# Zero fill of the sorted rows moved from the first stage into the first attention, and context values projected in blocks of 128 rows instead of 77

## What is computed

```python
x = x + xattn0(ctx, ctx, layernorm(x), mask)      # 16 heads of 32, weights shared by the heads
x = x + bit_linear_conv_ffn(layernorm(x))
x = x + xattn1(layernorm(x), ctx, ctx)            # 16 heads of 64
x = x + moe(layernorm(x))                         # tokens sorted by expert, two per token

# inside both cross attentions
K = ctx @ Wk.T ;  V = ctx @ Wv.T                  # 616 = 8*77 context rows
out = softmax(Q @ K.T * scale) @ V @ Wo.T

# inside moe
x_sort = x_flat[token_ids_sort]
w13_out = ragged_dot(x_sort, moe_w13, group_sizes)
```

## Time and profile before

| what | value |
|---|---|
| three runs | 3473.69, 3482.69, 3483.56 us |
| span of the profiled execution | 3475.7 us |
| `context` | 0 to 157 us |
| `attention` 0 | 157 to 644.7 us |
| PE busy / DVE busy, whole kernel | 2708.8 / 1980.7 us |
| PE busy in the last 26 us of `context` | 0.00 us |

### The profile page before, as it was taken

One profiled execution on the slowest core, in us unless ns is written; L12 is line 12 of the kernel. 1 busy time (PEld: TensorE's weight loads), 2 busy tenths in 40 slices (PEclk: granted clock), 3 DMA queues, 4 the chain that ended last, 5 costly groups with the idle time before them and its releaser, 6 DMA issues. The chain is left out here.

```text
span 3475.7 us, 44833 instructions
## 1 busy us (share of the span) xinstructions
PE 2708.8 (78%) x14170; PEld 1390.6 (40%) x14171; DVE 1980.7 (57%) x2814; ACT 1157.9 (33%) x1751; POOL 934.7 (27%) x739
## 2 busy tenths in 40 slices
PE   7578888446656647888888831999999999999980
PEld 4245555212222214444555310454444445444440
DVE  3287777689999996666666463223333332333225
ACT  2133333266656535555555332111111111111110
POOL 0001010046756751111111025002233350550007
PEclk9789999678877878999999775999999999999995
DMA  9800000100000010000000145001222230320018
GB/s 383 130 30 6 11 5 8 49 0 1 1 0 0 1 51 9 8 8 11 7 7 8 37 145 179 31 30 61 72 69 82 86 107 30 103 91 30 30 43 275
DMA packets 146005, 194.13 MB, mean 56 GB/s; under 512 B 85073, under 2 KB 85073, under 8 KB 145417
## 3 DMA queue, kind: packets, MB, share of 16 engines
q1 hardware_dynamic: 120569, 102.96, 10.6%
q0 software_dynamic: 25360, 90.21, 7.5%
HBM read 122.65 MB, written 70.48 MB: 56 GB/s over the span
## 5 line engine op out<-in xcount | busy, mean ns | idle before, releaser
L1789 PE MATMUL e_gate_up<-weights,e_x_t 128*128 x3456 | 771.5, 380 | 1.4 <-ACT e_x_t L1843 1.4
L1789 PEld LDWEIGHTS e_gate_up<-weights,e_x_t 128*128 128x128 bf16 x3456 | 332.6, 98 | 377.0 <-issue 4.3
L1876 DVE TENSOR_TENSOR e_mid<-e_gate,e_gate_up 128x512 f32<-128x512 f32 x144 | 99.0, 687 | 644.0 <-ACT e_gate L1849 644.0
L1809 PE MATMUL e_out<-weights,e_mid_t 128*128 x1728 | 384.7, 379 | 1.1 <-DVE e_mid_t L1889 1.1
L1849 ACT ACTIVATE e_gate<-e_gate_up 128x512 f32<-128x512 f32 x144 | 86.0, 597 | 684.0 <-PE e_gate_up L1789 684.0
L546 PE MATMUL a_turn<-a_wo,a_mixed_t 128*128 128x512 bf16 (+1 forms) x1024 | 284.2, 434 | 2.3 <-DVE a_mixed_t L804 1.7
L1035 PE MATMUL f_product<-f_xq_t,f_w 128*128 128x512 bf16 x512 | 168.2, 468 | 118.7 <-DVE f_padded L1236 89.9
L1809 PEld LDWEIGHTS e_out<-weights,e_mid_t 128*128 128x128 bf16 x1728 | 169.1, 98 | 204.8 <-issue 1.2
L479 POOL TENSOR_TENSOR a_probs<-a_e,a_probs 128x616 bf16<-128x616 f32 x64 | 85.6, 1353 | 545.1 <-ACT a_probs L713 545.1
L989 POOL TENSOR_TENSOR f_shared<-f_shared 128x512 f32<-128x512 f32 x128 | 180.8, 1413 | 171.0 <-DVE f_shared L1268 171.0
L978 POOL TENSOR_TENSOR hidden<-hidden,f_up_row 128x512 f32<-128x512 f32 x128 | 199.1, 1565 | 88.2 <-ACT f_up_row L1181 88.2
(11 more groups left out here) (234 smaller groups left out, 4485.5 us busy)
## 6 DMA issues: line engine op xcount, KB each, us to landing
raw_weights<-in_w POOLq DMA_DIRECT2D x72, 512.0 KB, 4.0
sorted_x<-c_zero_row POOLq DMA_DIRECT2D x1, 18432.0 KB
e_x_rows<-sorted_x SPq DMA_DIRECT2D x72, 256.0 KB, 2.7
sorted_y<-e_y_rows SPq DMA_DIRECT2D x72, 256.0 KB, 2.0
raw_weights<-in_w SPq DMA_DIRECT2D x24, 512.0 KB, 4.1
x<-in_x SPq DMA_DIRECT2D x4, 2048.0 KB, 49.1
out<-x SPq DMA_DIRECT2D x32, 256.0 KB, 4.2
hidden<-in_w_t SPq DMA_DIRECT2D x1, 4096.0 KB, 13.6
```

Of the source, the lines that this page charges most:

```text
L1789: last = nc.tensor.matmul(gate_up[half][:, part, :], x_t[:, u, a, k, :], plan.weights13[:, bass.ds(expert % 2, 1), b, k, col:col + 512], s ...
L1809: last = nc.tensor.matmul(out[:, :], mid_t[:, a, j, :], plan.weights2[:, bass.ds(expert % 2, 1), b, j, :], start=(j == 0 and a == b == 0), ...
L1876: nc.vector.tensor_tensor(mid[:, half, :], gate[:, half, :], gate_up[half][:, 1, :], ALU.mult).then_inc(mid_made, 1)
```

## The change

There are two edits in `context` and one in `attention` 0.

The zero row, the fill and the wait for it leave `context`. In `attention` 0 POOL clears its own `zero_row` behind its two other memsets, adds the bias to the eight tiles of batches 0 and 1, issues the fill, adds the bias to the other 24 tiles and waits for the fill at its end.

The values of a layer are computed in blocks over the 616 rows of all batches: four of 128 and one of 104, where there were eight of 77. The list `products` has 13 entries of layer 0 (16 before) and 26 of layer 1 (32 before). Each block of values is stored when its last column piece is done: five stores where there was one for layer 0, and five for each of the two parts in layer 1.

```diff
-    values = [sb("values0", [KEYS, B, CH[0] * P]), sb("values1", [KEYS, 2, B, CH[1] * P], BF16)]
+    values = [sb("values0", [P, BLOCKS, CH[0] * P]), sb("values1", [P, 2, BLOCKS, CH[1] * P], BF16)]
...
-            for b in range(B):
+            for r in range(BLOCKS):
                 for lo in range(0, CH[n] * P, 512):
-                    products.append(("values", n, b, lo, lo + 512))
+                    products.append(("values", n, r, lo, lo + 512))
...
-                elif kind == "values" and i == B - 1 and hi == CH[n] * P:
+                elif kind == "values" and hi == CH[n] * P:
                     wait_out(sp, u)
                     for a in parts:
-                        source = values[0][:, :, :] if a is None else values[1][:, a, :, :]
-                        target = values_out[0] if a is None else values_out[1][a]
-                        sp.dma_start(target.rearrange("b k n -> k b n"), source).then_inc(stored, 16)
+                        source = values[0][:, i, :] if a is None else values[1][:, a, i, :]
+                        target = (values_out[0] if a is None else values_out[1][a]).rearrange("b k n -> (b k) n")
+                        sp.dma_start(target[i * P:i * P + rows_of(i), :], source[0:rows_of(i), :]
+                                     ).then_inc(stored, 16)
                         made += 1
             sp.wait_ge(stored, 16 * made)
-            sp.wait_ge(cleared, 16)
...
-            nc.gpsimd.memset(zero_row[:, :], 0.0).then_inc(zeroed, 1)
-            pool.wait_ge(zeroed, 5)
-            pool.dma_start(sorted_x.rearrange("(s p) d -> p s d", p=P),
-                           zero_row[:, :].unsqueeze(1).broadcast_to([P, SLOTS, 2 * D])).then_inc(cleared, 16)
...
-                        last = nc.tensor.matmul(out[0:KEYS, :], ctx_t[:, k, i * KEYS:(i + 1) * KEYS],
+                        last = nc.tensor.matmul(out[0:rows_of(i), :], ctx_t[:, k, i * P:i * P + rows_of(i)],
                                                 wv[:, k, lo:hi], start=(k == 0), stop=(k == KD - 1))
...
+                nc.gpsimd.memset(zero_row[:, :], 0.0).then_inc(row_zeroed, 1)
                 pool.wait_ge(small_in, 16)
-                with pool.Fori(0, NT) as t:
+
+                def add_bias(t):
                     pool.wait_ge(xn_made, t + 1)
                     nc.gpsimd.tensor_tensor(core.x[:, t, :], core.x[:, t, :], bo[:, :], ALU.add
                                             ).then_inc(bo_added, 1)
+
+                for t in range(2 * TPS):
+                    add_bias(t)
+                pool.wait_ge(row_zeroed, 1)
+                pool.dma_start(w["sorted_x"].rearrange("(s p) d -> p s d", p=P),
+                               zero_row[:, :].unsqueeze(1).broadcast_to([P, SLOTS, 2 * D])).then_inc(cleared, 16)
+                with pool.Fori(2 * TPS, NT) as t:
+                    add_bias(t)
+                pool.wait_ge(cleared, 16)
```

More of the change, by code:

```diff
@@ L127, in norm_on_act, with context @@
     nc.scalar.activation(core.norm_tmp[:, 1, :], core.norm_tmp[:, 0, :], ACT.Sqrt).then_inc(root_ready, 1)
-def context(nc, core, x_in, w, keys_out, values_out, sorted_x):
+def context(nc, core, x_in, w, keys_out, values_out):
     QUARTERS = 4
@@ L140, in context @@
     BANKS = 8
+    FULL_BLOCKS, REST = divmod(BK, P)
+    BLOCKS = FULL_BLOCKS + 1
     with ExitStack() as stack:
@@ L146, in context @@
         ctx_t = sb("ctx_t", [P, KD, BK])
-        zero_row = sb("zero_row", [P, 2 * D], BF16)
         wk4 = sb("wk4", [DH, 4, DH])
@@ L155, in context @@
         keys = [sb("keys0", [P, CH[0], BK]), sb("keys1", [P, 2, CH[1], BK], BF16)]
-        values = [sb("values0", [KEYS, B, CH[0] * P]), sb("values1", [KEYS, 2, B, CH[1] * P], BF16)]
+        values = [sb("values0", [P, BLOCKS, CH[0] * P]), sb("values1", [P, 2, BLOCKS, CH[1] * P], BF16)]
         x_in_sb = [sem(f"x_in{q}") for q in range(QUARTERS)]
-        cleared = sem("cleared")
         small_in = sem("small_in"); wv_in = sem("wv_in"); ctx_in = sem("ctx_in"); layer1_in = sem("layer1_in")
@@ L171, in context, with rows_of @@
                 products += [("keys", n, c, 0, 512), ("keys", n, c, 512, BK)]
-            for b in range(B):
+            for r in range(BLOCKS):
                 for lo in range(0, CH[n] * P, 512):
-                    products.append(("values", n, b, lo, lo + 512))
+                    products.append(("values", n, r, lo, lo + 512))
         in_layer0 = sum(1 for product in products if product[1] == 0)
+        def rows_of(r):
+            return P if r < FULL_BLOCKS else REST
         def wait_out(engine, u):
@@ L259, in _ @@
                     elif n == 0:
-                        last = nc.tensor.matmul(out[0:KEYS, k * P:(k + 1) * P],
-                                                ctx_t[:, k, i * KEYS:(i + 1) * KEYS], wv_bd[:, :],
+                        last = nc.tensor.matmul(out[0:rows_of(i), k * P:(k + 1) * P],
+                                                ctx_t[:, k, i * P:i * P + rows_of(i)], wv_bd[:, :],
                                                 start=True, stop=True)
                     else:
-                        last = nc.tensor.matmul(out[0:KEYS, :], ctx_t[:, k, i * KEYS:(i + 1) * KEYS],
+                        last = nc.tensor.matmul(out[0:rows_of(i), :], ctx_t[:, k, i * P:i * P + rows_of(i)],
                                                 wv[:, k, lo:hi], start=(k == 0), stop=(k == KD - 1))
@@ L278, in _ @@
                 else:
-                    target = values[1][:, 0, i, lo:hi] if n == 1 else values[0][:, i, lo:hi]
-                    nc.scalar.activation(target, src[0:KEYS, :], ACT.Copy).then_inc(product_copied, 1)
+                    r = rows_of(i)
+                    target = values[1][0:r, 0, i, lo:hi] if n == 1 else values[0][0:r, i, lo:hi]
+                    nc.scalar.activation(target, src[0:r, :], ACT.Copy).then_inc(product_copied, 1)
         @block.vector
@@ L307, in _ @@
                 else:
-                    nc.vector.tensor_tensor(values[1][:, 1, i, lo:hi], src[0:KEYS, :], values[1][:, 0, i, lo:hi],
+                    r = rows_of(i)
+                    nc.vector.tensor_tensor(values[1][0:r, 1, i, lo:hi], src[0:r, :], values[1][0:r, 0, i, lo:hi],
                                             ALU.subtract).then_inc(product_low, 1)
@@ L361, in attention @@
             bias = sb("bias", [P, TPS, KEYS])
+            zero_row = sb("zero_row", [P, 2 * D], BF16)
         else:
@@ L403, in attention @@
             scores_read = sem("scores_read")
+            row_zeroed = sem("row_zeroed"); cleared = sem("cleared")
             normed = probs_ready
@@ L1956, in program @@
         sorted_y = scratch("sorted_y", [ROWS, D])
-        context(nc, core, t["x"], t, keys, values, sorted_x)
+        context(nc, core, t["x"], t, keys, values)
         with ExitStack() as both:
@@ L1963, in program @@
             attention(nc, core, 0, dict(keys=keys[0], values=values[0], mask=t["mask"], wo_t=t["wo0_t"], bo=t["bo0"],
-                                        ahead=ahead))
+                                        ahead=ahead, sorted_x=sorted_x))
             ffn(nc, core, t, hidden, w1_in)
```

## The result

| | before | after |
|---|---|---|
| median of the runs | 3483.12 us (4 runs) | 3431.82 us (4 runs, 3431.24 to 3436.17) |
| ratio, 95% interval | | 0.9865 (0.9849 to 0.9881) |
| span of the profile | 3475.7 us | 3429.5 us |

The account below looks back on a forecast made before the run. A chain of x loads stretched by the fill, key stores and values stores was taken to end the first stage. Its 47.2 us less, with 0 paid in attention, gave a 3428.5 us span, 3435.5 us median; range 3419 to 3453.

Parts of the forecast that it names:

- The fill stretched the loads of x: First stage: without the fill's 45.3 us of full DMA engines, weights land at 19.2 us and x by 39.3.
- Key stores, 20 at 2.87 us and 3 us of values, SP done with them at 99.8 us: First stage, SP's queue: 20 key stores take 57.4 us behind x, to 96.7 us, with values stores after.
- bound of 3.10: First stage: far bound for one key store in us, 62.0 us for all 20 instead of 57.4.
- Values stores: End of the first stage: 3.78 MB in 128-partition blocks take 9.1 us at 417 GB/s, 13.9 at 272.
- 4.0 remain: End of the first stage: last landing and barrier, the 13.3 us behind the last issue less 9.3 of transfer.
- Compute: First stage: with fewer blocks PE is done at 90.3 us, compute at about 91.7, with 18 us of slack.
- the old blocks' stage end at 124 us: First stage with the fill moved but 8 blocks kept: PE would end at 113.6 us, the stage near 124.
- The fill in the attention: First attention: fill issued at 217.9 us of the old trace, runs 45.3 us under cover, cost 0 us.
- rival D: First attention: POOL held up at the fill's issue by busy DVE; at 165 us of issue, 3495 us; chance 0.03.
- 7.0 us between span and median: Whole kernel: the median of the runs lay this far above the profile's span, and was carried over to the forecast.
- Rival B: First attention pays back 18 us through clock falls or late transfers; net gain 29 us, 3454 us; chance 0.12.

Follow-up runs that it names:

- e_keys: Changed kernel with keys kept in DRAM as features by 616 columns, so key stores have 128 long runs instead of 1024 short ones; 0.9807 of before.
- e_valpool: Changed kernel with layer 1's ten values stores issued on POOL's queue instead of behind the key stores on SP's; 0.9851 of before.
- e_blocks: Changed kernel with the fill back in the first stage, so only the blocks of 128 rows differ from before; 0.9988 of before.
- e_fill: Changed kernel with the old 8 blocks of 77 rows and three values stores, so only the fill's move differs from before; 0.9902 of before.
- e_split: Changed kernel with the fill in eight pieces of 2.36 MB, one behind the bias of each batch; 0.9875 of before.
- e_twoqueues: Changed kernel with the low halves' eight key stores of layer 1 on POOL's queue, the high halves' eight on SP's; 0.9884 of before.

## Why the prediction was right

**The fill stretched the loads of x.** Predicted: weights at 19.2 us, x at 39.3. PE's keys start at 20.94 without a wait and run through in one piece, which they can only if DVE gets its quarters of x in time; DVE has the first at 25.02 us, where 24.2 was predicted, and waits for none after it. SP is free of x at 26 us. Right.

**Key stores, 20 at 2.87 us and 3 us of values, SP done with them at 99.8 us.** SP was done at 98.10. The single store was 3.08 us, near the bound of 3.10, but the first ones had gone out under the loads of x, so that the 16 began at 48.73 us and not near 54. Right as a sum, with two errors that cancel. e_keys shows that it is the short runs that are paid for.

**Values stores, the step that was mis-sized.** "At 417 GB/s the 3.78 MB take 9.1 us" and "4.0 remain" put 10.0 us behind the last key store (6.0 for layer 1 and the 4.0). It was 18.0. The rate was nearly right: once the values ran alone they moved 385 GB/s, and at that rate layer 1's 2.52 MB take 6.6 us, where I had 6.0. On the number of engines the Trainium skill (page "DMA: Bandwidth & Descriptors", section "Why a DMA increments its semaphore by 16 and not by 1") agrees with both shares. The rates go with it: 385 / 272 is 1.42, and 16 / 11 is 1.45. Wrong was that I counted the end of SP's issue as the end of the key transfers. The values had their rate only at 108 us, 9.9 us behind their first issue: until about 102 us there were only key runs, and until 108 the last of them together with the first values, at 121 GB/s for both:

```profile
102.00:108.00 6.00, 0.00 (x0) 0.00 (x0) 0.00 (x0) 0.00 (x0) 0.00 (x0) 0.50 1.21 121
```

e_valpool, which goes round the queued keys, is 9.6 us shorter. The rows of the kernel before had this wait in them. 17.8 us pass there from the first of the two stores to the end; I took the 13.3 behind the end of the second one's issue, put them behind the last key store, and so dropped 4.5 us. Of the 8.0 us that were missing the rate makes 0.6; the other 3 us or so are key runs that cleared more slowly than before, and why they did isn't shown. The stage so ended at 116.06 us instead of 109.8.

**Compute.** Predicted 90.3 us for PE, measured 90.06. That the blocks pay only once the fill is gone is shown from both sides: e_blocks (stage 3.5 us longer than before) and e_fill (10.4 us longer than after, compute at the end). I had put the old blocks' stage end at 124 us; it was 126.50.

**The fill in the attention.** I took 0 us, with bounds of 0 and 2 for the mask. DVE waited 2.51 us for it, and the iteration was 3.4 us longer. I had sized the fill at 45.3 us, from the 417 GB/s of a stretch that also had loads; alone it moved 368, and landed in 55.9. The place was right, the mask of batch 2: it is the only load that is waited for there. e_split shows it: with pieces that wait is gone, and the iteration is 2.8 us shorter. That the 3.8 us by which the first attention got longer are all this wait isn't shown, since kernels with the same fill differ by as much. Of rival D, nothing: POOL's issue took 3.08 us beside a busy DVE.

**What I hadn't priced.** 7.8 us came back in `ffn` and `attention` 1. These windows have the same columns as the earlier trace rows. They are 30 us at the end of the second attention, of the kernel before and then of the changed one:

```profile
1923.00:1953.00 30.00, 26.66 (x86) 11.20 (x87) 6.01 (x8) 9.36 (x12) 1.43 (x2) 0.50 0.00 1
```

```profile
1889.00:1919.00 30.00, 25.72 (x130) 12.06 (x128) 8.71 (x13) 10.45 (x14) 0.71 (x1) 0.94 0.00 1
```

PE ran at half its clock (1.2 GHz) for the whole stretch before, and near full clock (2.4 GHz) after. PE has the same gap of 3.20 us just there in both kernels:

```profile
1923.22 1.90 PE L495 MATMUL a_flip<-ident_bf,a_probs 128*77 128x128 bf16 x16 [3.20 <-POOL a_probs L479]
```

```profile
1888.50 1.45 PE L509 MATMUL a_flip<-ident_bf,a_probs 128*77 128x128 bf16 x16 [3.20 <-POOL a_probs L493]
```

From the gap's end to the next stage it is 52.1 us before and 41.8 after. What differs is where the granted clock falls: at 1922.9 us, 0.3 us before the gap's end, in the kernel before, and at 1889.0, 0.5 us behind it, in the changed one. It is so in all eleven profiles. In the five with a long fall (30.7 or 34.1 us) it comes 0.3 to 1.0 us before PE works again, in the six with the short one (3.4 us) 0.5 us after. So the length goes with how the kernel's gap lies to the fall, which no part of the prediction could have placed; that it came out as a gain is luck.

So the 47.2 us predicted and the 46.2 of the spans agree because errors cancel: 6.2 us too much for the first stage and 3.8 for the attention, against 9.0 from untouched stages (7.8, and 1.2 from `routing` on, which the second profiles don't repeat). The two stages that the change touches gave 37.2. In the forecast of the median a fourth term was off: I carried over 7.0 us between span and median, and it was 2.3. Rival B named the clock as a cost in the first attention; it came as a gain, in another stage.

## What to carry to other kernels

A long transfer costs what shares the DMA engines with it, so look at the other queue: the end of an issue isn't the end of its data, and what must land last belongs on a queue without a backlog. Read the rate of a transfer in a window in which nothing else moves. When such a transfer is moved under compute, list the small loads that are due in it, and cut it in pieces where one has little slack. And ask of each edit what it is worth without the other: a saving on a hidden engine becomes real only when what hid it has gone.

## What the runs showed of the hardware

- A store of 128 partitions with 1024 runs of 154 bytes took 3.1 us, one of the same bytes in 128 runs was never the end of the stage. With two queues sharing such stores the engines were at 0.65 in a stretch where only SP's were left.
- Stores of 2 KB rows from SBUF to DRAM, with nothing beside them, moved 272 GB/s from 77 partitions at a DMA share of 0.71, and 385 GB/s from 128 at 1.01. While short key runs queued ahead of them were still on their way, both together moved 121 GB/s. The fill alone moved 368 GB/s at 0.99, loads and fill together 417 at 1.03.
- A mask of 154 KB landed 24 us after its issue beside the fill on the other queue; the median of the eight was 2.5 us. With the fill in eight pieces it wasn't waited for.
- Around the same gap of 3.20 us on PE at the end of the second attention, the granted clock stayed at 1.2 GHz for 3.4 us in some kernels, for 30.7 in others and 34.1 in e_valpool and e_twoqueues. It was long where the fall came before the gap's end, and short where it came after. It repeated in second profiles of two kernels. It is worth 8 to 10 us. Why the two lengths differ so much is open.
